# A residual stream kept in DRAM: stored as bf16 instead of f32, with two SBUF buffers in turn instead of one

## What is computed

```
x = x + ln(rwkv(ln(x)))
y = ln(x)
for l in (0, 1):
    h = shift_token(y)                 # second half of the features one token late
    q, k, v = split(h @ wqkv[l])       # 8 heads of 64, l2norm, rotary
    y = y + local_attention(q, k, v) @ wo[l]   # windows of 512 and the one before
    h = ln(shift_token(y)) * lg[l] + lb[l]
    a, g = split(h @ w1[l] + b1[l])
    y = y + (a * gelu(g)) @ w2[l] + b2[l]
x = x + ln(y)
```

## Time and profile before

| what | us |
|---|---|
| median of 3 runs | 5560.03 (5553.22 to 5602.08) |
| the profiled execution | 5560.03 |
| its span, slowest core (core 3) | 5558.4 |
| spans of the other cores | 5495.1 to 5547.4 |
| PE, DVE, ACT busy in the span | 2857.7, 2152.3, 1065.4 |

### The profile page before, as it was taken

How to read it: one execution, slowest core, us unless ns; L and a number is a source line. 1 busy time by engine, 2 the same in 40 slices (tenths; PEclk the granted TensorE clock), 3 DMA queues, 4 the chain that set the end, 5 groups by cost and what they waited for, 6 DMA issues and landing times.

```text
span 5558.4 us, 43456 instructions; the slowest of 8 cores (5495.1 to 5558.4 us)
## 1 busy us (share of the span) xinstructions
PE 2857.7 (51%) x12752; PEld 1346.4 (24%) x12752; DVE 2152.3 (39%) x4565; ACT 1065.4 (19%) x2053; POOL 38.2 (1%) x46
## 2 busy tenths in 40 slices
PE   3333323222365655564865783556565548667822
PEld 2222222211122222221322231222222213223311
DVE  3566666664242424242332231424242423322334
ACT  0222222221040313131111110313131321111100
POOL 0000000000000000000000000000000000000000
PEclk9666666655656565555977896565555558778855
DMA  6000000002301010103500004010101035000022
GB/s 97 0 1 0 1 0 0 1 31 67 67 1 46 1 46 1 46 1 76 88 31 31 31 1 88 1 46 1 46 1 46 1 68 96 31 31 31 1 76 91
DMA packets 92663, 182.15 MB, mean 33 GB/s; under 512 B 2064, under 2 KB 20752, under 8 KB 92304
## 3 DMA queue, kind: packets, MB, share of 16 engines
q1 hardware_dynamic: 62256, 118.07, 6.9%
q0 software_dynamic: 30176, 61.32, 6.8%
HBM read 177.78 MB, written 54.53 MB: 42 GB/s over the span
## 4 chain that ended last, share of the span: by engine, by line
PE 35%; DVE 34%; ACT 9%; issue 9%; DMA 9%; another core or an unknown queue 2%; DVEq 2%; ACTq 0%; POOL 0%; SPq 0%; POOLq 0%
PE pb_l L1564 6%; PE pa_l L1039 5%; PE pa_l L1308 4%; ACT PRB_l L1210 4%; DMA YBF<-ysp 3%; DVE RRF L1198 3%; PE pba_l L1514 3%; PE pbg_l L1528 3%; PE pb_l L1528 3%; PE pb_l L1514 3%; DMA ysp<-YBF 2%; DVE PRB_l L1233 2%; DVEq L194 2%; PE pb L637 2%
## 5 line engine op out<-in xcount | busy, mean ns | idle before, releaser
L1154 PE MATMUL pa_l<-KR_l,QH_l 64*128 64x512 bf16 x256 | 149.0, 582 | 429.6 <-ACT PRB_l L1214 402.5
L1564 PE MATMUL pb_l<-HACT_l,W2P_l 128*128 128x512 bf16 x1408 | 319.9, 390 | 42.5 <-DVE YBF L1580 29.1
L1210 ACT ACTIVATE PRB_l<-pa_l,RRF 128x512 bf16<-128x512 f32 x256 | 176.4, 689 | 748.3 <-DVE RRF L1206 748.3
L637 PE MATMUL pb<-XKk,WR 128*128 128x256 bf16 x512 | 73.3, 316 | 380.2 <-ACT KF L671 380.2
L1514 PE MATMUL pba_l<-HB_l,W1I_l 128*128 128x512 bf16 x704 | 179.7, 401 | 154.6 <-DVE HB_l L1491 154.6
L1308 PE MATMUL pa_l<-OH_l,WOF_l 64*128 64x512 bf16 x512 | 220.9, 626 | 32.3 <-DVE YBF L1322 27.1
L1014 PE MATMUL pa_l<-WQKV_l,HQ_l 128*128 128x512 bf16 x256 | 75.2, 466 | 310.4 <-DVE YLC L1005 165.9
L1055 ACT ACTIVATE SQB_l<-pa_l 128x512 bf16<-128x512 f32 x64 | 38.3, 598 | 948.2 <-PE pa_l L1039 943.5
L1242 PE MATMUL pbf_l<-CBF,PRB_l 128*128 128x128 bf16 x1280 | 188.4, 313 | 47.4 <-DVE PRB_l L1233 47.4
L1227 DVE TENSOR_TENSOR RRF<-RRF 128x1 f32<-128x1 f32 x256 | 40.9, 160 | 426.6 <-ACT PRB_l L1214 426.6
L1564 PEld LDWEIGHTS pb_l<-HACT_l,W2P_l 128*128 128x128 bf16 x1408 | 140.0, 100 | 222.5 <-issue 68.1
(11 more groups left out here) (223 smaller groups left out, 4520.6 us busy)
## 6 DMA issues: line engine op xcount, KB each, us to landing
YBF<-ysp SPq DMA_DIRECT2D x16, 2048.0 KB, 11.4
ysp<-YBF SPq DMA_DIRECT2D x16, 2048.0 KB, 7.2
W1I_l<-w1i POOLq DMA_DIRECT2D x10, 2048.0 KB, 54.2
W2P_l<-w2p POOLq DMA_DIRECT2D x10, 1024.0 KB, 89.7
ysp<-KF SPq DMA_DIRECT2D x8, 1024.0 KB, 4.4
RT_l<-rot SPq DMA_DIRECT2D x8, 1024.0 KB, 14.0
YF<-ysp SPq DMA_DIRECT2D x4, 2048.0 KB, 11.2
out<-OT SPq DMA_DIRECT2D x16, 512.0 KB, 2.7
```

What stands on the lines that cost most here:

```text
L637: return e.matmul(pslot(bank0, oc), W[:, kc, oc * 128:oc * 128 + 128], dst[:, kc, :], start=(kc == 0), stop=(kc == CH - 1))
L1210: return e.activation(PRB[:, par, 0:512], sA[:, 0:512], AF.Exp, bias=nm, accum_out=s1c)
L1564: return e.matmul(PB_[oc4][:], W2P[:, j, oc * 128:oc * 128 + 128], HACT[:, j, :], start=(j == 0), stop=(j == NJ - 1))
```

## The change

`ysp`, the tile `YBF`, the column `YLC` and the tile `YF4` become bf16, so each transfer of y has half the bytes. `YBF` becomes one of the two halves of `YB2` [128, 2, 8, 512], chosen by `fb % 2`; each half has its own store semaphore, and a load waits for the last store from its own half, no longer for the store of the block before. The first stage's result is written to `XKv` (bf16, a tile of the rwkv part that is free by then) instead of `KF`. The sum y + update is therefore rounded to bf16 each time it is stored.

```
-    ysp_h = dt("ysp", [128, CH, T])
+    ysp_h = nc.dram_tensor("ysp", [128, CH, T], BF16).ap()
...
-                            return e.tensor_tensor(KF[:, c, :], XC[:, c, :],
+                            return e.tensor_tensor(XKv[:, c, :], XC[:, c, :],
                                                    PBS[7][:, 0:TB], ALU.mult)
...
-                                 ysp_h[:, :, col:col + TB], KF[:],
+                                 ysp_h[:, :, col:col + TB], XKv[:],
...
-        YBF = sb("YBF", [128, CH, FT], F32)
-        YLC = sb("YLC", [128, CH, 2], F32)
+        YB2 = sb("YB2", [128, 2, CH, FT], BF16)
+        YLC = sb("YLC", [128, CH, 2], BF16)
...
-            t_store = None
+            t_store_par = [None, None]
             for fb in range(NF):
                 col = fb * FT
-                w_l = [t_prev_writes]
-                if t_store is not None:
-                    w_l.append(t_store)
+                ypar = fb % 2
+                YBF = YB2[:, ypar]
+                w_l = (list(t_prev_writes)
+                       if isinstance(t_prev_writes, list)
+                       else [t_prev_writes])
+                if t_store_par[ypar] is not None:
+                    w_l.append(t_store_par[ypar])
...
-                t_store = p.dma("y", f"yw{l}a",
-                                ysp_h[:, :, col:col + FT], YBF[:],
-                                waits=[t_yb])
+                t_store_par[ypar] = p.dma("y", f"yw{l}a{ypar}",
+                                          ysp_h[:, :, col:col + FT], YBF[:],
+                                          waits=[t_yb])
...
-            t_prev_writes = (p.dsem[f"yw{l}a"], p.dma_cnt[f"yw{l}a"])
+            t_prev_writes = [(p.dsem[f"yw{l}a0"], p.dma_cnt[f"yw{l}a0"]),
+                             (p.dsem[f"yw{l}a1"], p.dma_cnt[f"yw{l}a1"])]
...
-             nc.sbuf_tensor("YF4", [128, CH, FT], F32) as YF4, \
+             nc.sbuf_tensor("YF4", [128, CH, FT], BF16) as YF4, \
```

More of the change, by code:

```diff
@@ L993, in emit_layer, with hq1, hq2 @@
                              waits=[(p.sem["v"], p.cnt["v"])])
-                def hq1(e):
+                def hq1(e, YBF=YBF):
                     return e.tensor_copy(HQ[:, 0:4, :], YBF[:, 0:4, :])
                 p.add("v", hq1, waits=[t_yl])
-                def hq2(e):
+                def hq2(e, YBF=YBF):
                     return e.tensor_copy(HQ[:, 4:8, 1:FT],
@@ L1003, in emit_layer, with ylup @@
                 p.add("v", hq3)
-                def ylup(e):
+                def ylup(e, YBF=YBF):
                     return e.tensor_copy(col2d2(YLC, 0),
@@ L1334, in emit_layer @@
             t_pa_done = p.tok("pe")
-            t_prev_writes = (p.dsem[f"yw{l}a"], p.dma_cnt[f"yw{l}a"])
+            t_prev_writes = [(p.dsem[f"yw{l}a0"], p.dma_cnt[f"yw{l}a0"]),
+                             (p.dsem[f"yw{l}a1"], p.dma_cnt[f"yw{l}a1"])]
             if dbg_dump:
                 t_prev_writes2 = p.dma("y", "dby", dby_h[f"a{l}"], ysp_h,
-                                       waits=[t_prev_writes])
-                t_prev_writes = t_prev_writes2
+                                       waits=list(t_prev_writes))
+                t_prev_writes = [t_prev_writes2]
             pa.close()
@@ L1385, in emit_layer, with c1, c2 @@
             p.add("v", zYL2)
-            t_store = None
+            t_store_par = [None, None]
             for fb in range(NF):
                 col = fb * FT
-                w_l = [t_prev_writes]
-                if t_store is not None:
-                    w_l.append(t_store)
+                ypar = fb % 2
+                YBF = YB2[:, ypar]
+                w_l = (list(t_prev_writes)
+                       if isinstance(t_prev_writes, list)
+                       else [t_prev_writes])
+                if t_store_par[ypar] is not None:
+                    w_l.append(t_store_par[ypar])
                 t_yl = p.dma("y", f"yb{l}", YBF[:],
                              ysp_h[:, :, col:col + FT], waits=w_l)
-                def c1(e):
+                def c1(e, YBF=YBF):
                     return e.tensor_copy(HB[:, 0:4, :], YBF[:, 0:4, :])
                 p.add("v", c1, waits=[t_yl])
-                def c2(e):
+                def c2(e, YBF=YBF):
                     return e.tensor_copy(HB[:, 4:8, 1:FT],
@@ L1405, in emit_layer, with sq1 @@
                 t_cb = p.tok("v")
-                def sq1(e):
+                def sq1(e, YBF=YBF):
                     return e.activation(SQ2[:, 0:4, :], YBF[:, 0:4, :],
@@ L1409, in emit_layer, with sq2_ @@
                 p.add("s", sq1, waits=[t_yl, (p.sem["v"], p.cnt["v"])])
-                def sq2_(e):
+                def sq2_(e, YBF=YBF):
                     return e.activation(SQ2[:, 4:8, 1:FT],
@@ L1467, in emit_layer, with ap1 @@
                     if c < 4:
-                        def ap1(e, c=c):
+                        def ap1(e, c=c, YBF=YBF):
                             return e.tensor_tensor(TMP1[:], YBF[:, c, :],
@@ L1500, in emit_layer, with ylup2 @@
                     p.add("v", lambda e: e.engine_nop(), waits=[t_dw1])
-                def ylup2(e):
+                def ylup2(e, YBF=YBF):
                     return e.tensor_copy(col2d2(YLC, 1),
@@ L1578, in emit_layer, with yup @@
                         oc = half * 4 + oc4
-                        def yup(e, oc=oc, oc4=oc4):
+                        def yup(e, oc=oc, oc4=oc4, YBF=YBF):
                             return e.scalar_tensor_tensor(
@@ L1585, in emit_layer @@
                 t_yb2 = p.tok("v")
-                t_store = p.dma("y", f"yw{l}b",
-                                ysp_h[:, :, col:col + FT], YBF[:],
-                                waits=[t_yb2])
+                t_store_par[ypar] = p.dma("y", f"yw{l}b{ypar}",
+                                          ysp_h[:, :, col:col + FT], YBF[:],
+                                          waits=[t_yb2])
             t_pb_done = p.tok("pe")
-            t_prev_writes = (p.dsem[f"yw{l}b"], p.dma_cnt[f"yw{l}b"])
+            t_prev_writes = [(p.dsem[f"yw{l}b0"], p.dma_cnt[f"yw{l}b0"]),
+                             (p.dsem[f"yw{l}b1"], p.dma_cnt[f"yw{l}b1"])]
             if dbg_dump:
-                t_prev_writes = p.dma("y", "dby", dby_h[f"b{l}"], ysp_h,
-                                      waits=[t_prev_writes])
+                t_prev_writes = [p.dma("y", "dby", dby_h[f"b{l}"], ysp_h,
+                                       waits=list(t_prev_writes))]
             t_gate_prev = [t_pb_done, p.tok("v"), p.tok("s"), p.tok("g")]
@@ L1634, in build @@
                 if stage >= 2:
+                    wly = (list(t_prev_writes)
+                           if isinstance(t_prev_writes, list)
+                           else [t_prev_writes])
                     t_ly = p.dma("y", "yf4", YF4[:],
                                  ysp_h[:, :, col:col + FT],
-                                 waits=[t_prev_writes, t_lx])
+                                 waits=wly + [t_lx])
                     def c4a(e):
```

2 lines of the change are left out of this document (1 added, 1 removed).

## The result

The forecast was 5360 us, a ratio of 0.964 to the 5560 us of before. Measured side by side, the changed kernel takes 0.9633 of the time of before (95% interval 0.9572 to 0.9695). The profile read here is of another execution of the same kernel, of 5366.1 us (the first run among the experiments), whose slowest core is core 5.

What follows compares the result with a forecast made beforehand. The bound was taken to be uncovered waits at block boundaries, engines idle while y is stored and the next columns load. Savings of 61 + 29 + 32 + 37 + 28 + 13 = 200 us from 5560.0 gave 5360 us, range 5312 to 5425.

Steps and rivals of the forecast that it cites:

- The loads are not prefetched: At block boundaries: the load stands behind the store in SP's list, so only the wait for the store's landing goes.
- Term 1: Six boundaries inside stage B: wait falls from 18.2 to 9.1 us, with copies 10.2 us saved each, 61 us.
- The copies: DVE's two copies at each block's start: 1.23 us falls to 0.69 each, the shifted one too, 0.53 saved by each.
- Term 2: Three boundaries inside stage A, layer 1: wait falls from 19.5 to 11.0 us, with copies 29 us saved.
- Term 3: Three boundaries inside stage A, layer 0: wait falls from 22.2 to 12.5 us, with copies 32 us saved.
- Term 4: Two starts of stage B: the wait halves from 35.63 to 18 us, with copies 37 us saved.
- It just fits: Start of stage B: the last weights, landing at 2717 for a need at 2737, still arrive in time when that moves 18.7 us forward.
- Term 5: The end: shorter last store, four shorter loads of y and four faster copies to bf16, together 28 us saved.
- Term 6: Starts of stage A: weights issued sooner after a shorter last store, with fewer bytes beside them, together 13 us saved.
- one after the other: Rival at the boundaries: store, copies and load drain in turn, all starts paid; 161 us saved, 5399 us, chance 0.23.
- side by side: Rival at the boundaries: reads and writes overlap, 6.5 us in stage B; 241 us saved, 5319 us, chance 0.17.
- The clock: Rival in stage B: a quarter of the matmuls stay at the low clock level, 241 us, time 5601 us, chance 0.02.

Runs made afterwards that it cites:

- one-buffer kernel: The changed kernel with one y buffer again, still bf16, so each load waits for the store before it to land; ratio to before 0.971, fastest run 5369.8 us.

## Why the prediction was right

The forecast by its steps:

- **The loads are not prefetched.** Right. The load goes 0.74 us behind the store, and the kernel with the load moved shows what was missed: twelve waits of 0.
- **Term 1.** Wait forecast 9.1, found 9.6. The working had one start of 1.6 us, 2.8 for the store's bytes and 4.9 for the load's, less a little overlap. At the boundary shown the load took 8.8 us from its issue, with the store beside it, against 5.9 alone in the one-buffer kernel: the store added 2.9, its bytes' price. The overlap that I took off wasn't there. 0.5 us by 6 are the 3 us.
- **The copies.** 0.694 us, shifted or not. The Trainium skill is of two minds: "VectorE: DVE Perf Modes", section "Mode 2×_1P", asks for 4-byte alignment, "Vector Engine (DVE) Microarchitecture Reference", section "5.1 Performance modes — why throughput varies by op and dtype", says that it makes no difference. These rows side with the latter: one shape, one element off, no loss.
- **Term 2.** The wait forecast for a boundary of stage A in layer 1 was 1.0 us too low. Of that 0.5 comes from stage B's 9.6; I had given stage A 1.9 us above stage B, and it pays 2.4 (12.0 to 9.6). The step that failed is "0.8 for the late issue": the load goes 2.2 us later behind the store than in stage B, and from its issue it takes 8.8 to 8.9 us where stage B's takes 8.3 to 8.9, so nearly all of the 2.4 us is lateness and little of it the 1.1 that I gave the copies. Issuing earlier buys little, though, because the load then takes 10.3 to 10.8 us; only holding back copies and rotary table brings 9.6. The rotary table, 1 MB right behind the load, has no term in the prediction, and its share isn't known.
- **Term 3.** 1.7 us too low: 4.6 us above stage B where I had given 3.4. In layer 0 the load itself takes 10.6 to 11.4 us on core 5. I put a part of this down to the other core, and the eight cores of this execution speak for it: cores 0, 1, 4 and 5, which by their own timelines reach these boundaries 2.0 to 3.9 us from their neighbour (0 with 1, 4 with 5), wait 13.5 to 14.4 us on average; cores 2, 3, 6 and 7, 4.5 to 7.9 us from theirs, 12.1 to 12.8; and in layer 1, where all are 9 us or more apart, all wait 12.0 to 12.4. No run set these offsets on purpose, and with copies and table held back no such difference is seen (9.1 to 10.0), so it is shown only as far as this goes.
- **Term 4.** 17.8 for a forecast of 18. Both the late core (35.63 to 17.61) and the early one (22.27 to 10.99) halved. The late core stayed the disturbed one. Core 4's load was issued at 2548.79, 3.6 us ahead of its own weights, and had landed by 2554.8; core 5's, issued at 2556.89, 3.1 us ahead of its own, took 11.65 us, so its own weights don't explain the difference. If the two cores began together, it ran beside core 4's weights. All eight starts of stage B in this execution (four pairs of neighbours, two layers) agree: in seven the later core waits 16.7 to 18.0 us and the earlier 10.9 to 11.6, at offsets of 5.6 to 24.7 us; in the eighth the two are 2.2 us apart, and both are quick (11.8 and 12.0). The Trainium skill ("HBM Reference", section "Specifications (TRN2)") says that two cores of a pair share the bandwidth, and these rows agree. It isn't tested: no run stopped the neighbour. Which core of a pair is late isn't fixed (of cores 2 and 3 it was 3 before and is 2 now), so the prediction's sign "core 3 gaining less than core 2" can't be read. "It just fits" held too, with 15 us to spare, and the kernel with stage B's first load moved shows that it wasn't much.
- **Term 5.** 4.6 us too low. The last store saved 2.8 as worked out, the copy to bf16 1.06 each; a load of y takes 5.6 to 5.8 us, not 6.0; and the loads of x, whose bytes are unchanged, are 7.48, 7.49 and 7.80 us in the last three blocks of the chain of before and about 6.4 now. That is mostly the core I read: on the other seven cores of before the same loads average 6.8 us, and in the kernel with f32 and the prefetch in stage A, whose end is as before, 6.7 on all eight. Over all cores the four waits of the end fell from 79.6 to 55.0 us, with the copies 28.8 for a forecast of 28. The surplus on the slowest core is luck.
- **Term 6.** 10.1 us for 13 from slowest core to slowest core, and 13.1 on the average of the eight cores (141.7 to 128.7), but the split was wrong: layer 0 gave 8.6 on average where I had 4.4, layer 1 gave 4.5 (0.5 on the slowest) where I had 8.5. The failed step is that the earlier issue of layer 1's weights, which came as forecast (11.71 to 6.0 us at L975), would bring PE's start forward by as much; MSK's landing took longer instead. Why stays open.

Of the rivals, one after the other (5399) is out in stage B, where 10.8 us would have stood, and so is side by side (5319, 6.5 us). The one-buffer kernel is the serial case: 10.96 us. The clock didn't move: in a block of stage B the windows view gives 0.83 for the 0.82 of the earlier trace rows.

```profile
2907.00:3092.00 185.00, 128.26 (x548) 55.03 (x548) 52.77 (x89) 23.07 (x29) 0.00 (x0) 0.83 0.08 23
```

The errors of the terms were -3, -3, -5, +1, +5 and -3, and 2 us are unplaced, so that the sum of 200 was 194. The mechanism was right: what the time gained is the wait for y at every boundary. That the total came this close is in part luck: the +5 is an accident of the cores compared, and the time itself, over the six executions, has a 95% interval of some 70 us.

## What to carry to other kernels

A second buffer prefetches nothing while the load stands behind the store in the issuing engine's list: here it brought 1.4 us a boundary in stage B, and moving the load's issue brought the other 9.6. Read the issuing queue's order before counting on overlap. Halving the bytes of a transfer that stands bare on the path pays by its own slope, with all start-up costs left; and each wait that goes uncovers the next (weights, a copy inside SBUF), so look up how early these land before counting the whole wait as gain.

## What was not expected of the hardware

- A store that has a load 0.7 us behind it lands after about 6.0 us instead of 4.7, and the load after 8.3 to 8.9 instead of 5.9, both of 1 MB on one queue: what takes 10.7 us one after the other takes 9.4. A store and a load hardly overlap here.
- Two copies of 512 KB inside SBUF and a load of 1 MB (the rotary table) beside the load of y make it 10.3 to 10.8 us long when the store is beside it too, against 8.3 to 8.9 with the store alone. The shares of copies and table weren't tested apart.
- The core of a pair that comes later to the start of stage B waits 17 us for a load that the earlier one has after 11, in seven of eight cases; the eighth, 2.2 us apart, shows neither.
